# Making the folded value-output matrix N for two batches at once from 64-row matmuls

## The reference, cut to what matters

```
q = layernorm(layernorm(x), ln2) @ Wq ; k, v = split(layernorm(ctx, ln1) @ Wkv)   # 16 heads of 64
q = q * (1 + scale) + shift
attn = softmax(q k^T / 8)                       # over 64 context rows, per head
x = x + (attn v, heads joined) @ Wout           # x: 16 batches x 1024 rows x 512
x = x + tanh(layernorm(x) @ (W A1 A2) + bias)
```

## Time and profile before

| | us |
|---|---|
| median of three runs (2051.54 to 2052.84) | 2052.41 |
| profiled execution, first to last instruction | 2049.4 |
| PE busy | 2024.3 |
| DVE busy | 1523.8 |
| ACT busy | 1320.3 |
| POOL busy | 1342.0 |
| TensorE granted clock, mean share | 0.999 |

### The profile page before, as it was taken

The page is one execution under the profiler, slowest core; times in us unless marked ns, Lnnn a source line. Parts: engine busy times, 40 slices in busy tenths (PEclk is TensorE's granted clock), DMA queues, the critical chain, the costliest instruction groups (busy, mean ns, idle before and its releaser), DMA issues.

```text
span 2049.4 us, 31334 instructions
## 1 busy us (share of the span) xinstructions
PE 2024.3 (99%) x9168; PEld 1679.8 (82%) x9168; DVE 1523.8 (74%) x2416; ACT 1320.3 (64%) x3005; POOL 1342.0 (65%) x1463
## 2 busy tenths in 40 slices
PE   8998999999999999999999999999999999999998
PEld 6887878888888888888888888888888888888887
DVE  7567777776777777677777777777777777777776
ACT  4465667666766667666666667666666666666654
POOL 2136767767676776767676776767577676767564
PEclk9999999999999999999999999999999999999999
DMA  7657978889787887878788787878767576666653
GB/s 256 196 184 219 269 226 245 247 231 253 215 229 206 222 222 209 225 202 233 195 229 223 206 224 205 229 201 216 209 186 210 175 206 181 201 184 191 178 169 118
DMA packets 502489, 431.53 MB, mean 211 GB/s; under 512 B 54832, under 2 KB 408240, under 8 KB 502320
## 3 DMA queue, kind: packets, MB, share of 16 engines
q1 hardware_dynamic: 502320, 429.54, 74.3%
HBM read 251.33 MB, written 178.06 MB: 210 GB/s over the span
## 4 chain that ended last, share of the span: by engine, by line
PE 94%; DVE 1%; DMA 1%; ACT 1%; SPq 1%; issue 1%; POOL 0%; DVEq 0%; ACTq 0%
PE bank L161 38%; PE bank L1126 23%; PE bank L166 19%; PE bank L1129 11%; PE bank L830 1%; PE bank L829 1%; DMA stage_more<-ffn_wT_dram 0%; PE bank L827 0%; SPq L306 0%; DMA kv_scratch<-area 0%; ACT bank L388 0%; DMA p_moved<-p_scratch 0%; ACT M_hi L392 0%; PE bank L511 0%; DMA p_scratch<-area 0%
## 5 line engine op out<-in xcount | busy, mean ns | idle before, releaser
L1403 POOL TENSOR_TENSOR area<-area,row_max 128x256 f32<-128x256 f32 x512 | 353.7, 711 | 147.8 <-DVE row_max L1269 147.8
L1126 PE MATMUL bank<-N_hi,pT_hi 128*128 128x512 f32 x1024 | 398.8, 389 | 3.0 <-ACT pT_hi L1172 1.7
L161 PE MATMUL bank<-M_lo,xT_hi 128*128 128x512 f32 x1024 | 398.7, 389 | 0.0
L161 PE MATMUL bank<-M_hi,xT_hi 128*128 128x512 f32 x1024 | 398.6, 389 | 0.0
L1126 PE MATMUL bank<-N_lo,pT_hi 128*128 128x512 f32 x1024 | 398.5, 389 | 0.0
L1172 ACT CAST pT_hi<-turned 128x512 fp32r<-128x512 f32 x256 | 159.1, 621 | 330.4 <-DVE turned L1286 330.4
L1410 POOL TENSOR_TENSOR area<-area,row_inv 128x512 f32<-128x512 f32 x256 | 269.0, 1051 | 114.3 <-DVE row_inv L1278 114.0
L1427 POOL TENSOR_TENSOR area<-area 128x512 f32<-128x512 f32 x127 | 166.0, 1307 | 240.6 <-ACT area L1211 240.5
L1275 DVE TENSOR_REDUCE row_sum<-area 128x8 f32<-128x512 f32 x256 | 174.4, 681 | 167.7 <-ACT area L1167 166.7
L1295 DVE TENSOR_TENSOR pT_lo<-turned,pT_hi 128x512 fp32r<-128x512 f32 x256 | 196.5, 768 | 118.0 <-ACT pT_hi L1172 117.9
L166 PE MATMUL bank<-M_hi,xT_lo 128*128 128x512 f32 x1024 | 273.8, 389 | 0.1
(11 more groups left out here) (178 smaller groups left out, 3916.8 us busy)
## 6 DMA issues: line engine op xcount, KB each, us to landing
p_scratch<-area SPq DMA_DIRECT2D x256, 256.0 KB, 2.6
p_moved<-p_scratch SPq DMA_DIRECT2D x512, 128.0 KB, 4.2
area<-x_dram SPq DMA_DIRECT2D x128, 256.0 KB, 4.5
area<-x_turned_dram SPq DMA_DIRECT2D x128, 256.0 KB, 4.0
x_scratch<-area SPq DMA_DIRECT2D x127, 256.0 KB, 3.0
x_moved<-x_scratch SPq DMA_DIRECT2D x508, 64.0 KB, 3.4
y_dram<-area SPq DMA_DIRECT2D x127, 256.0 KB, 3.4
land<-m_scratch SPq DMA_DIRECT2D x120, 256.0 KB, 2.7
```

What stands on the lines that cost most here:

```text
L161: mm = eng.matmul(ps, sh, mv, start=(n == 0), stop=False)
L1126: pe.matmul(O_ps[:], st(pT_hi, k), n_cols(mv, k), start=(k == 0 and mv is N_hi), stop=False)
L1403: last = pool.tensor_tensor(s, s, row.to_broadcast([P, 2, 4, J2]), ALU.subtract)
```

## The change

From batch 4 on, N is made for batches b0 and b0+1 (b0 even) together, one pair in each of eight slots: t = 8(b0-1)+2+p. These are slots 26 to 33, 42 to 49, 58 to 65, 74 to 81, 90 to 97 and 106 to 113, 48 in all. For a pair, head h's v of both batches stands as 64 rows by 128 columns (64 columns to a batch), head 0 in partitions 0 to 63, head 1 in 64 to 127; the matmul of head h uses only its 64 rows and writes bank h. The six matmuls alternate between the halves. For the odd batch the heads' order in the rows of N is swapped, and p is written in the matching order. Results are copied to a stage in SBUF (where `Wo` was) and split into N in the slot with m = 1, as before. `Wo` is stored to DRAM in slots 10 to 25 (16 DMAs of 256 KB) and its pair is loaded again for each stacked slot (two DMAs of 256 KB).

```diff
+        STACKED = 4
+        stacked_at = {TPB * (b0 - 1) + 2 + p: (b0, p) for b0 in range(STACKED, B, 2) for p in range(PAIRS)}
+        def load_v2(sp, b0, p):
...
+            sp.dma_start(v2_raw[0:DH, :].rearrange("e (b j) -> e b j", b=2), even[:, b0:b0 + 2, :]).then_inc(s_vin, 16)
+            for i in range(2):
+                sp.dma_start(v2_raw[DH:P, i * CTX:(i + 1) * CTX], odd[:, b0 + 1 - i, :]).then_inc(s_vin, 16)
+        def load_wo2(sp, b0, p):
...
+            if n:
+                sp.wait_ge(s_n, n_tiles(n, 0))
+            for h in range(2):
+                sp.dma_start(wo2[h][:].bitcast(F32), wo_scratch[p, h]).then_inc(s_wo2, 16)
+        def v2_split_hi(act, b0, p):
...
+            act.copy(v2_hi[:], v2_raw[:]).then_inc(s_vh, 1)
+        def v2_split_lo(pool, b0, p):
...
+            pool.tensor_tensor(v2_lo[:], v2_raw[:], v2_hi[:].bitcast(F32), ALU.subtract).then_inc(s_vp, 1)
+        def n2_pe(pe, b0, p):
+            pe.wait_ge(s_wo2, 32 * n + 32)
+            pe.wait_ge(s_vp, STACKED + n + 1)
...
+            for i, (v, w) in enumerate(((v2_hi, wo2[0]), (v2_hi, wo2[1]), (v2_lo, wo2[0]))):
+                for h in range(2):
+                    own = slice(h * DH, (h + 1) * DH)
+                    mm = pe.matmul(n2_ps[h][:], v[own, :], w[own, :], start=(i == 0), stop=(i == 2))
+        def n2_evacuate(eng, copy, b0, p, h):
+            eng.wait_ge(s_n, n_tiles(n, h) + 1)
...
+            copy(stage_of(b0 + h, p)[0:DH], n2_ps[h][0:DH, :])
+            copy(stage_of(b0 + 1 - h, p)[DH:P], n2_ps[h][DH:P, :]).then_inc(s_nev, 1)
+        def n2_hi(act, b):          # slot m = 1: eight copies stage -> N_hi
+        def n2_lo(dve, b):          # slot m = 1: eight subtractions -> N_lo
...
@@ slot_sp
-            if m == 0 and 0 < t < T:
+            if m == 0 and 0 < t < TPB * STACKED:
                 load_v(sp, t // TPB)
...  after write_p(0):
+            if t + 1 in stacked_at:
+                load_v2(sp, *stacked_at[t + 1])
+            if 10 <= t < 26:
+                store_wo(sp, t - 10)
...  at the end of the slot:
+            if t + 1 in stacked_at:
+                load_wo2(sp, *stacked_at[t + 1])
@@ slot_pe, inside the output of tile t-2
                 tile("BC"[q])
+                if t in stacked_at and q == 0:
+                    n2_pe(pe, *stacked_at[t])
...
-            if m == 1 and 1 < t < T:
+            if m == 1 and 1 < t < TPB * STACKED:
                 fold_n_pe(pe, t - 1, range(8), ...)
@@ slot_act: v2_split_hi after the second half of p's high part; n2_evacuate(..., 0) before evacuate("C")
@@ slot_dve, after the residual add
             sum_tile("C")
+            if t in stacked_at:
+                n2_evacuate(dve, dve.tensor_copy, *stacked_at[t], 1)
@@ slot_dve, slots with m == 0: diag_lo (the low part of bdv) only for batches below 4
@@ slot_pool: v2_split_lo before subtract_maximum(0)
```

More of the change, by code:

```diff
@@ L84, in build @@
         N_hi, N_lo = sb("N_hi", PAIRS * D, F32R), sb("N_lo", PAIRS * D, F32R)
+        with nc.sbuf_tensor("n_stage", [P, 2 * PAIRS * D], F32) as n_stage:
+            pass
         Wo_hi, Wo_lo = sb("Wo_hi", PAIRS * D, F32R), sb("Wo_lo", PAIRS * D, F32R)
         W3_hi, W3_lo = sb("W3_hi", DC * D, F32R), sb("W3_lo", DC * D, F32R)
+        with ExitStack() as over:
+            v2_raw = over.enter_context(nc.sbuf_tensor("v2_raw", [P, P], F32))
+            v2_hi, v2_lo = (over.enter_context(nc.sbuf_tensor(f"v2_{n}", [P, P], F32R)) for n in ("hi", "lo"))
+            wo2 = [over.enter_context(nc.sbuf_tensor(f"wo2_{i}", [P, D], F32R)) for i in range(2)]
         bdv = sb("bdv", PAIRS * 2 * P, F32R)
@@ L674, in v_prepare_act, with heads_swapped @@
             last.then_inc(s_vh, 1)
+        STACKED = 4
+        stacked_at = {TPB * (b0 - 1) + 2 + p: (b0, p) for b0 in range(STACKED, B, 2) for p in range(PAIRS)}
+        nth_pair = lambda b0, p: PAIRS * (b0 - STACKED) // 2 + p
+        stage_of = lambda b, c: n_stage[:, (b % 2 * PAIRS + c) * D:(b % 2 * PAIRS + c + 1) * D]
+        n2_ps = banks[2:4]
+        n_tiles = lambda n, h: PAIRS * STACKED + 2 * n + h
+        WST_STORES, WO_STORES, V_LANDED = 16 * 16, 16 * 16, 16 * STACKED
+        def heads_swapped(b):
+            return b >= STACKED and b % 2 == 1
@@ new lines, in store_wo @@
+        def store_wo(sp, i):
+            part, q = i // 8, i % 8
+            sp.dma_start(wo_scratch[q:q + 1, part].rearrange("p e d -> e p d"),
+                         (Wo_hi, Wo_lo)[part][:, q * D:(q + 1) * D].bitcast(F32).rearrange("e (p d) -> e p d", p=1)).then_inc(s_wstw, 16)
+        def load_v2(sp, b0, p):
+            n = nth_pair(b0, p)
+            sp.wait_ge(s_vp, STACKED + n)
+            if n == 0:
+                sp.wait_ge(s_n, PAIRS * STACKED)
+            even, odd = kv_scratch[1, p, 0:DH], kv_scratch[1, p, DH:P]
+            sp.dma_start(v2_raw[0:DH, :].rearrange("e (b j) -> e b j", b=2), even[:, b0:b0 + 2, :]).then_inc(s_vin, 16)
+            for i in range(2):
+                sp.dma_start(v2_raw[DH:P, i * CTX:(i + 1) * CTX], odd[:, b0 + 1 - i, :]).then_inc(s_vin, 16)
@@ new lines, in n2_evacuate @@
+        def n2_evacuate(eng, copy, b0, p, h):
+            n = nth_pair(b0, p)
+            eng.wait_ge(s_n, n_tiles(n, h) + 1)
+            eng.wait_ge(s_nl, PAIRS * (b0 - 1) + p + 1)
+            if n == 0:
+                eng.wait_ge(s_wstw, WST_STORES + WO_STORES)
+            copy(stage_of(b0 + h, p)[0:DH], n2_ps[h][0:DH, :])
+            copy(stage_of(b0 + 1 - h, p)[DH:P], n2_ps[h][DH:P, :]).then_inc(s_nev, 1)
+        def n2_hi(act, b):
+            act.wait_ge(s_o, TPB * b)
+            for c in range(PAIRS):
+                act.wait_ge(s_nev, 2 * nth_pair(b - b % 2, c) + 2)
+                act.copy(n_cols(N_hi, c), stage_of(b, c)).then_inc(s_nh, 1)
@@ L680, in build @@
+        def n2_lo(dve, b):
+            for c in range(PAIRS):
+                dve.wait_ge(s_nh, PAIRS * b + c + 1)
+                dve.tensor_tensor(n_cols(N_lo, c), stage_of(b, c), n_cols(N_hi, c).bitcast(F32), ALU.subtract).then_inc(s_nl, 1)
         m_where = lambda c: ((c // 2) % 4, 2 * (c // 8) + c % 2)
@@ L879, in load_land @@
             at_least(sp, s_ll, l)
-            if b and j == 1:
+            if 0 < b < STACKED and j == 1:
                 sp.wait_ge(s_vp, b + 1)
@@ L1033, in slot_sp @@
                     src = p_scratch[u % 2].rearrange("(g r) (a w) -> a r g w", g=4, a=4)[a]
-                    sp.dma_start(p_moved[a * J2:(a + 1) * J2, :].rearrange("p (g w) -> p g w", g=4), src).then_inc(s_pr, 16)
+                    to = a ^ 2 if heads_swapped(u // TPB) else a
+                    sp.dma_start(p_moved[to * J2:(to + 1) * J2, :].rearrange("p (g w) -> p g w", g=4), src).then_inc(s_pr, 16)
             store("D", t - 1)
@@ L1083, in slot_sp @@
                 load_land(sp, 6)
[L1084 removed]
+            elif m == 0 and t < TPB * STACKED:
                 load_land(sp, t + 1)
+            if t + 1 in stacked_at:
+                load_wo2(sp, *stacked_at[t + 1])
         def slot_pe(pe, t, m):
@@ L1100, in slot_pe @@
                         pe.wait_ge(s_ll, t - 4 + 4 * q)
-                    elif m == 2 and t > 2:
+                    elif m == 2 and 2 < t < TPB * STACKED:
                         pe.wait_ge(s_nl, t + 3 + q)
@@ L1245, in slot_act @@
                 ln1_stats(act, 3, 3)
+            if t in stacked_at:
+                n2_evacuate(act, act.copy, *stacked_at[t], 0)
             evacuate("C")
@@ L1248, in slot_act @@
                 pT_hi_part(0, t - 1)
-            if m == 0 and 0 < t < T:
+            if m == 0 and 0 < t < TPB * STACKED:
                 v_prepare_act(act, t // TPB)
-            if m == 1 and 1 < t < T:
+            if m == 1 and 1 < t < TPB * STACKED:
                 fold_n_act(act, t - 1, range(8))
+            elif m == 1 and TPB * STACKED < t < T:
+                n2_hi(act, t // TPB)
             if t == 5:
@@ L1328, in slot_dve @@
                     dve.wait_ge(s_thl, h + 1)
-                    dve.tensor_tensor(y, y, last_half(hid_last, h), ALU.add).then_inc(s_yl[h], 1)
+                    dve.tensor_tensor(y, y, last_half(hid_last, h), ALU.add).then_inc(s_yl, 1)
             elif tile_of(t - 5):
@@ L1391, in slot_dve @@
                 pT_lo_part(0, t - 1)
-            if m == 0 and 0 < t < T:
+            if m == 0 and 0 < t < TPB * STACKED:
                 diag_lo(dve, bdv, s_vh, s_vp, t // TPB)
-            if m == 1 and 1 < t < T:
+            if m == 1 and 1 < t < TPB * STACKED:
                 fold_n_dve(dve, t - 1, range(8))
+            elif m == 1 and TPB * STACKED < t < T:
+                n2_lo(dve, t // TPB)
         def slot_pool(pool, t, m):
```

25 lines of the change are left out of this document (23 added, 2 removed).

## The result

The kernel before took 2052.62 us (four runs, 2051.54 to 2054.11), the changed kernel 2072.78 us (four runs, 2071.86 to 2076.18): ratio 1.0099, 95% interval 1.0085 to 1.0113. It is 20 us slower. The forecast of 2054 was 19 us too low; the time lies inside the range (2042 to 2074), and slower was the likeliest of the three outcomes.

What follows compares the result with a forecast made beforehand. PE was taken to bound the kernel up to slot 89, DVE's round after it. Terms -38.1 - 1.6 - 8.6 + 32n + 16e, plus 0.5, gave +1.5 on 2052.4: 2054 us, range 2042 to 2074.

Steps and rivals of the forecast that it cites:

- The matmuls taken away, -38.1: PE before slot 89: seven folds of 5.44 us go, -38.1 us, against 32 stacked slots at n each.
- DVE's first read, -1.6: Slot 89: without `bdv`, DVE's first read comes 2.92 us after the slot's start, 1.64 us sooner.
- n = 1.04: PE time added per stacked slot by six 64-row matmuls: 0.72 us side by side plus 0.32 for both ends.
- (a): Six matmuls: halves run serially or weights reload at each end, n from 1.12 on, 2064 to 2074 us; chance 0.26.
- 1.42: Value of n in us by the skill's rule if weights are reloaded at the change of shape; gives +13.6 us.
- e = 1.0: DVE time in us added per stacked slot by two copies out of PSUM, after part falls into holes; bounds 0.5 and 1.65.
- "Up to slot 89 PE is": Before slot 89 PE is the last engine: 233.9 us over two batches against DVE's 232.7.
- The late stretch, -8.6 + 16e: Slots 89 to 127: DVE's round is longer, 535.0 + 16e against 543.6 us; new PE waits for pT_hi or pT_lo.
- "PE's new wait is met.": Stacked slots: `wo2` lands 2.7 us after issue, needed 8 us into PE's slot, so PE need not wait.
- Hidden at nothing: ACT's copies, POOL's v2 subtraction, SP's extra DMAs and Wo's stores in slots 10 to 25 were each priced at 0.
- (c): DVE in stacked slots: e is 1.5 because v2 lands late or holes aren't filled, 2069 us; chance 0.10.
- (b): Six matmuls: clean overlap, no price for the change of shape, n = 0.72, 2046 us; chance 0.26.

Runs made afterwards that it cites:

- thin_split: Changed kernel with both halves of the splitting of N from batch 4 on made for only 8 of 512 columns; 2045.93 us, ratio 0.9963.
- evac_p: Changed kernel with DVE's two copies out of PSUM moved to ACT in the 42 stacked slots with m other than 1; 2073.52 us, ratio 1.0103.
- x_some: Changed kernel with the next x tile's splits moved ahead of the softmax only in slots where DVE lags after the splitting of N; 2064.94 us, ratio 1.0059.
- x_sp: x_some plus SP's loads of v2 and Wo issued ahead of p's first store, from the second pair on; 2052.76 us, ratio 0.9994.
- x_sp_pool: x_sp with two of the eight low-part subtractions of N moved from DVE to POOL from batch 4 on; 2054.52 us, ratio 0.9999.

## Why the prediction was right or wrong

**The matmuls taken away, -38.1, and DVE's first read, -1.6.** Right: in thin_split PE's slots are what these terms and n make them; the second measured -1.4.

**n = 1.04.** It measured 1.11 to 1.12, the edge from which on the prediction counted rival (a). The three steps are 0.68 to 0.70 (0.72 assumed), but each end costs about 0.21 instead of 0.16: the change of shape delays not one matmul but two, by 0.1 each (steps of 0.32 and 0.33 instead of 0.23). The Trainium skill, TensorEngine Tiling (Array Packing), Key Properties, says that a change of tiling empties TensorE. The trace agrees that it costs something (n is above 0.72). That weights are loaded again on top (1.42) did not happen.

**e = 1.0.** Late stacked reads are 1809.23 - 1794.80 = 14.43 apart, so e = 1.00 to 1.01.

**"Up to slot 89 PE is"** the last engine. This step failed. It compared 233.9 us of PE with 232.7 of DVE over two batches and took the larger. The larger sum gives the time only if the work of the other engine may come late and be made up later while nobody waits for it. From the trace after: xT_hi is ready 6.85 us after DVE's first read, so in a slot of 14.10 PE waits as soon as the read comes more than 14.10 - 6.85 = 7.2 us after the slot's start. The split made it 8.9. The trace before would have given it: there too xT_hi is ready 6.9 us after the read, and the fold of 5.44 us on PE stood in the same slot as the 4.93 on DVE and covered it. The change took the cover and left the 4.93. A reader can do this check as: lag before the split (4.2), plus DVE's round across it (19.9), less PE's slot (15.2), against 7.2. The round is no fixed number where DVE waits for PE in it: in evac_p the lag was 2.9, the round 21.2, and the result the same 8.9. thin_split bears the step out, since without the lump the kernel runs at the sum of the slots.

**The late stretch, -8.6 + 16e.** Right in size (7.0 for 7.4) and in cause, DVE's round. But PE's waits were looked for in the wrong place: not one is for pT_hi or pT_lo before slot 127. Slots 98, 99, 106 and 107 are 2.7, 1.7, 1.0 and 0.6 us longer than their kind, 6.0 where about 7 were expected per two batches. The 2.7 is mainly the wait for xT_hi, the 1.7 holds no wait but the lower clock of the last section, the 1.0 is mainly the wait for v2's low part, and in the 0.6 is one of 0.26 for xT_lo. The prediction also called itself wrong if stacked slots after slot 97 still had PE covered. Slots 108 to 113 have, at 14.71 or 14.72, and its own terms say so (13.60 + 1.04 is more than 13.43 + 1.0): DVE is the bound over two batches, not in each slot.

**"PE's new wait is met."** True in most of the 48 slots, not in the first two (3.1 us). Elsewhere it held in part because PE waited for x instead: x_some took this away and found 9.1 us of waits for Wo, the DMA landing 4.1 us after its issue where the prediction had taken 2.7 from another load. x_sp shows that SP's order was worth 12 us then.

**Hidden at nothing.** The stores of Wo in slots 10 to 25 cost nothing: from DVE's first read of slot 3 to that of slot 26 it is 353.6 us, and 354.0 before. ACT's copies and POOL's v2 part cost DVE nothing, since e came out without them, but v2's low part cost PE 1.9 us of waits, a term that the prediction put at nothing. That PE's waits outside the setup's longest add some 13 us before is a small misreading: they add 12.1.

**The rivals.** Neither (a) nor (c) happened, though the time is theirs: the halves overlap, e is 1.0, and the load of v2 made ACT wait in one of 48 slots, for 0.6 us. (b) would have needed n = 0.72. The time came near that of (a) and (c) for another reason, which stood in no rival; that the range held it is luck, owed to its width.

## What to carry to other kernels

When work is spread on the bound engine, look for the partner of that work that stays lumped on another: it was covered by the lump that leaves. Compare engines slot by slot with a running lag, and against the latest time at which the consumer needs the result, not over a period. And test a suspected wait by moving it only where it occurs: the same edit in all slots cost 17 us, most of it ahead of the first stacked slot, where nothing lagged; in the lagging slots it gained 8.

## What the runs showed of the hardware

A wait of PE may cost more than itself. After the longest wait for xT_hi in the late stretch (2.11 us, slot 98) the granted clock was half for some 3 us; the columns are us, PE busy, then weight loads, DVE, ACT, POOL, the clock, DMA share and GB/s:

```profile
1629.50:1632.00 2.50, 0.39 (x3) 0.03 (x1) 1.02 (x3) 2.34 (x6) 2.11 (x3) 1.00 0.42 105
1632.00:1634.00 2.00, 2.00 (x6) 1.62 (x7) 1.54 (x4) 0.34 (x1) 1.51 (x2) 0.65 0.45 131
1634.00:1636.00 2.00, 2.00 (x6) 1.40 (x6) 1.58 (x2) 0.28 (x1) 2.00 (x3) 0.50 0.64 198
1636.00:1638.00 2.00, 2.00 (x10) 1.66 (x9) 1.58 (x4) 1.46 (x3) 0.37 (x2) 0.99 1.01 307
```

The clock is 1.2 GHz instead of 2.4, and matmuls start 0.43 us apart. PE had stood idle for 2.11 us before it fell. At the boundary of slots 66 and 67, with a wait of 1.55, the matmuls behind it start 0.23 apart. The length of the wait alone does not decide it: in evac_p PE waits 2.08 and 2.07 us at the ends of slots 98 and 114, and the granted clock stays at 1.00. Here it made slot 99 1.7 us longer and cost the kernel little, as DVE was the bound: its reads behind slot 99 stay 13.43 apart.

A restart of PE after a wait costs about 0.1 us on top in the rows read: the first matmul lasts 0.50 and the next starts 0.33 behind it, as after a change of shape. And DVE's own round in the slots without N is not fixed: with the x splits early, the rounds before slots 100 to 105 took 13.02 us in x_sp instead of 13.43, with the same instructions on DVE: the wait of 0.31 for POOL's root is gone there, and the split of p that took 0.95 beside a POOL operation takes 0.69.

A subtraction on DVE lasts longer beside one on POOL: the last of DVE's six in slot 41 of x_sp_pool takes 1.78 us where it is 0.68 or 0.69 alone, and POOL's two take 1.49 and 1.74.
